# Gated cross- and self-attention block: cross batches and row tiles written out without engine loops, last shift and key copy moved forward

## The reference, cut to what matters

```python
def xattn(q, k, v):                    # q: layernorm(x) (32,100,512); k = v = context (32,722,512)
    qh, kh, vh = heads(q @ wq + bq), heads(k @ wk + bk), heads(v @ wv + bv)
    scores = softmax(einsum('bhqd,bhkd->bhqk', qh, kh), axis=-1)
    return concat(einsum('bhqk,bhkd->bhqd', scores, vh)) @ wo + bo

x = x + tanh(g_xattn[0]) * xattn(layernorm(x), ctx, ctx)
x = x + tanh(g_ffn[0]) * ffn(layernorm(x), g_info, W_qkv, W_proj, b_proj)
# ffn: q, k, v = x @ W_qkv; a cosine of each row's q with a guide row, averaged over heads and
# scaled to 0..1 over all rows, puts the row in one of two classes; attention with two key masks
```

## Time and profile before

| | us |
|---|---|
| median of 3 runs (lowest to highest) | 2854.22 (2852.57 to 2858.64) |
| profiled execution, its time | 2863.41 |
| profiled execution, its span | 2861.5 |
| PE busy in the span | 2642.9 (92%) |
| DVE, ACT, POOL busy | 1829.7, 1336.3, 372.3 |
| granted TensorE clock, mean | 0.961 |

### The profile page before, as it was taken

The page is one execution under the profiler, slowest core; times in us unless marked ns, Lnnn a source line. Parts: engine busy times, 40 slices in busy tenths (PEclk is TensorE's granted clock), DMA queues, the critical chain, the costliest instruction groups (busy, mean ns, idle before and its releaser), DMA issues. The chain is left out here.

```text
span 2861.5 us, 52305 instructions
## 1 busy us (share of the span) xinstructions
PE 2642.9 (92%) x17376; PEld 2361.2 (83%) x17376; DVE 1829.7 (64%) x2869; ACT 1336.3 (47%) x2994; POOL 372.3 (13%) x274
## 2 busy tenths in 40 slices
PE   5799999999999999999999999999949999579999
PEld 5689888988889888888988889888847777478887
DVE  6456676666766666666666766667646677436665
ACT  3235444554445554455544445444433444245654
POOL 0020110000110001110001100011013333100000
PEclk9899999999999999999999999999959999859999
DMA  5545444444544454444554445444339999788982
GB/s 174 176 127 122 120 107 119 118 113 120 119 112 111 120 122 117 105 119 111 121 121 117 119 103 124 119 120 102 92 111 177 187 199 201 152 168 191 194 186 76
DMA packets 367908, 380.02 MB, mean 133 GB/s; under 512 B 127950, under 2 KB 275310, under 8 KB 367726
## 3 DMA queue, kind: packets, MB, share of 16 engines
q1 hardware_dynamic: 317134, 358.18, 53.5%
q10 hardware_dynamic: 50592, 19.06, 3.4%
HBM read 162.57 MB, written 72.57 MB: 82 GB/s over the span
## 5 line engine op out<-in xcount | busy, mean ns | idle before, releaser
L649 DVE TENSOR_TENSOR c_parted<-c_prob,c_parted 128x600 fp32r<-128x600 f32 x512 | 400.9, 783 | 464.0 <-ACT c_prob L590 463.0
L586 ACT ACTIVATE c_parted<-c_pair 128x600 fp32r<-128x600 f32 x512 | 344.4, 673 | 375.5 <-PE c_pair L728 374.6
L635 DVE TENSOR_REDUCE c_peak<-c_pair 100x1 f32<-100x724 f32 x512 | 450.0, 905 | 76.8 <-PE c_pair L710 66.4
L532 POOL TENSOR_TENSOR c_ct_lo<-e_stage,c_ct_hi 128x722 fp32r<-128x722 f32 x128 | 224.7, 1757 | 1766.0 <-ACT c_ct_hi L561 1766.0
L742 PE MATMUL c_mix<-c_parted,c_v 128*66 128x200 f32 (+1 forms) x3072 | 379.0, 260 | 16.5 <-DVE c_q_stack L640 16.4
L728 PE MATMUL c_pair<-c_q_stack,c_k_stack 100*128 100x100 f32 (+1 forms) x3072 | 391.0, 264 | 0.0
L89 PE MATMUL c_work<-c_ct_hi,w_wk_hi 128*128 128x362 f32 (+1 forms) x1024 | 366.0, 357 | 20.1 <-POOL c_ct_lo L532 16.0
L728 PEld LDWEIGHTS c_pair<-c_q_stack,c_k_stack 100*128 100x128 f32 (+1 forms) x3072 | 375.2, 188 | 6.7
L568 ACT ACTIVATE c_v<-c_work 128x512 fp32r<-128x512 f32 x192 | 115.6, 602 | 527.2 <-PE c_work L91 527.2
L742 PEld LDWEIGHTS c_mix<-c_parted,c_v 128*66 128x66 f32 (+1 forms) x3072 | 327.2, 139 | 37.5 <-DVE c_q_stack L640 25.6
L89 PE MATMUL c_work<-w_wv_hi,c_ct_hi 128*128 128x512 f32 (+1 forms) x768 | 317.2, 413 | 34.4 <-issue 28.6
(11 more groups left out here) (162 smaller groups left out, 4155.6 us busy)
## 6 DMA issues: line engine op xcount, KB each, us to landing
c_k_stack<-c_k_hi SPq DMA_DIRECT2D x1024, 90.2 KB, 2.2
e_stage<-in_ctx SPq DMA_DIRECT2D x32, 1444.0 KB, 6.2
c_k_stack<-c_k_lo SPq DMA_DIRECT2D x512, 90.2 KB, 2.2
c_q_stack<-q_parts ACTq DMA_DIRECT2D x186, 100.0 KB, 3.2
mix_parts<-c_mixed SPq DMA_DIRECT2D x64, 200.0 KB, 3.2
r_parts<-mix_parts SPq DMA_DIRECT2D x50, 256.0 KB, 4.2
s_q_stack<-qk_parts SPq DMA_DIRECT2D x16, 800.0 KB
s_k_stack<-qk_parts SPq DMA_DIRECT2D x16, 800.0 KB
```

The costliest lines, as they stand in the source:

```text
L532: pool.tensor_tensor(ct_lo[odd][:, k, :], columns[:, k, :], ct_hi[odd][:, k, :], ALU.subtract).then_inc(ct_lo_done, 1)
L586: act.activation(parted[i % PR][:, :, 0, :].rearrange("p (a t) s -> p a t s", a=2), logits, ACT.Exp).then_inc(exp_hi_done, 1)
L635: dve.tensor_reduce(peak[:, i:i + 1], pair[i % 2][0:S, :, 0:HALF], AX.XY, ALU.max).then_inc(peak_done, 1)
L649: dve.tensor_tensor(p[:, :, 1, :], prob[i % 2][:], p[:, :, 0, :], ALU.subtract).then_inc(p_lo_done, 1)
```

## The change

Four edits. The three engine loops over batches, and those of PE, ACT and DVE over row tiles, become straight code: every batch and tile is written out, with constants where registers were. The fourth shift moves from behind scores 1 to the end of the front part, ahead of the first keys piece. In the row stage ACT's `keys(t)` moves ahead of `split_attn(t + 2)` and `query_root(t)`.

```diff
@@ front_plan
-    return plan + held[:2] + [("scores", 0, 0)] + held[2:]
+    return plan + held[:2] + [("scores", 0, 0)] + held[2:] + [("shift", KT - 1, 0)]
@@ batch_plan
-        if h == 1:
-            plan.append(("shift", KT - 1, 0))
@@ stage_cross, all_batches
-            body(0, 0, True, True)
-            with engine.Fori(0, B // 2 - 1) as u:
-                body(u * 2 + 1, 1, True)
-                body(u * 2 + 2, 0, True)
-            body(B - 1, 1, False)
+            for b in range(B):
+                body(b, b % 2, b < B - 1, b == 0)
@@ stage_rows, scalar, body
                 queries(t, before > 0)
+                keys(t)
                 if more_attn:
                     split_attn(t + 2)
                 query_root(t)
-                keys(t)
                 values(t, before > 0)
@@ stage_rows, scalar
-            with act.Fori(2, TILES - 2) as t:
+            for t in range(2, TILES - 2):
@@ stage_rows, vector
-            with dve.Fori(2, TILES - 2) as t:
+            for t in range(2, TILES - 2):
@@ stage_rows, tensor
-            with pe.Fori(2, TILES - 1) as t:
+            for t in range(2, TILES - 1):
```

## The result

| us | before | after |
|---|---|---|
| median of the runs (lowest to highest) | 2856.43 (2852.57 to 2858.64) | 2789.38 (2779.96 to 2798.39) |
| profiled execution, its span | 2861.5 | 2796.6 |
| mean granted clock in it | 0.961 | 0.965 |
| PE, DVE, ACT busy in it | 2642.9, 1829.7, 1336.3 | 2628.1, 1826.2, 1334.5 |
| first matmul of batch 1 to that of batch 31 | 1812.8 | 1748.8 |

The change is faster: ratio 0.976, 95% interval 0.9734 to 0.9785, 67 us between the medians. One single execution among all the kernels here, 3261.57 us at a granted clock of 0.74 with keys ahead alone, was far slower than every other and is left out of that kernel's numbers. The lower half of the table splits the profiled span by the matmuls that open and close each part; I call the last two the row stage and the self stage throughout, and every experiment is split in the same way.

A forecast was written before the change was run, and what follows sets the result against it. PE, busy 92% of the span, was taken to bound the kernel; 44.3 + 18.6 + 12.3 + 2.6 = 77.8 us gave 2785.6 from 2863.4, and most of the median's 9.2 us offset gave 2779, range 2765 to 2798.

The forecast's parts named there:

- Terms 1 and 2: Cross stage: straight code removes PE's branch stalls and half-clock stretches, 44.3 us; the earlier fourth shift ends mix 0's wait, 18.6.
- The zero for fetching straight code: All engines: fetching new instructions in every batch was costed at nothing, since an engine fetches ahead of its need.
- The fetch rival: Cross stage: DVE or ACT stops once per batch for a fetch, PE behind it; 122 us more, 2901; chance 0.03.
- the moved wait: Cross batches: PE waits as much further on, for DVE's maxima or stacked keys; batch stays 58.95, time 2798; chance 0.05.
- Term 3: Batch 31: mix 0's wait goes and the clock stays full, 2.0 + 9.3 + 1.0 = 12.3 us; bounds 0.9 to 14.
- one of my own signs of a wrong forecast: Profile after: the forecast is wrong if batch 31 is at granted clock 0.50.
- The rival of the slow tail: Batch 31: the clock falls all the same, from PE's small holes behind ACT's exps; 2790; chance 0.13.
- Term 4: Row stage: earlier keys let PE run ahead once until DVE's attention split, 2.6 us gained; bounds -2 to 13.
- The rival that all 13.2 us would go: Row stage: parts land faster once PE's stores leave earlier, so PE's whole wait for copies goes; 2768; chance 0.06.

The follow-up runs named there:

- keys ahead alone: Kernel before with only ACT's key copies moved ahead of its attention split in the row stage: 2858.65 us, ratio 1.0003.
- The batches alone: Kernel before with only the cross stage's batches written out, shift and row stage as before: 2806.33 us, ratio 0.9813.
- the full fill: The change with unread matmuls in batch 31, four ahead of mix 0 and two ahead of each other mix: 2792.61 us.
- TensorE alone: The change with cross batches written out on TensorE only, ACT and DVE given back their loops: 2787.70 us, ratio 0.9748.
- the two fills: The change with four unread matmuls ahead of mix 0 of batch 31, 2786.72 us; with two more ahead of each other mix, 2792.61 us.
- the warming: The change with 50 and 20 unread identity matmuls on TensorE around the self stage's first scores: 2782.67 us, ratio 0.9756.
- the two warmed kernels: Unread self-stage matmuls added to the change, 2782.67 us; and, with four ahead of batch 31's mix 0, to its cross stage with before's row stage, 2782.70 us.
- the cross stage alone: The change with before's row stage, its loops and its order of ACT's copies: 2776.12 us, ratio 0.9737.
- the kernel with less to load: The change, from row tile 4 on loading 8 of 128 partitions of the second set of mixed parts: 2773.69 us, ratio 0.9706.

## Why the prediction was right, and where it was not

The sign, the range (2765 to 2798) and the place of most of the gain were right; the median is 10 us above the forecast. By the steps:

**Terms 1 and 2**, the branches and the shift, 62.3 us between batches 1 and 31 (44.3 and 30 times 0.6): measured 64.0. The pieces bear out both sizes. The batches alone gave 45.3 against 44.3, the half-clock stretches with them, and from there the change took 18.7 more by the shift (1767.5 to 1748.8), 0.62 a batch. The zero for fetching straight code held too: the empty list of waits shows it. (I had called the 158 fetches of the earlier trace rows PE's; that row names a queue and no engine.) By the Trainium skill (Runtime: NRT & Kernel Launch, Instruction fetch mechanics) straight code crosses its blocks mostly unseen, and a taken branch to code outside the blocks at hand waits for its fetch. The trace agrees: no wait of PE in 30 straight batches, and 3.95 us for TensorE's taken branch. The fetch rival (2901) and the moved wait (2798) are out: all batches are at 58.3 to 58.6.

**Term 3**, batch 31, 12.3 us: in the profiled execution of the change 1.2, and there one of my own signs of a wrong forecast stands, batch 31 at 0.50. In the other kernels with the shift ahead it is 13. The step said that with the shift ahead mix 0 would have no gap and no reason would show for the clock to fall. A gap of 0.69 us stays, because I took the order of batch 14 for that of batch 31, where DVE's split of the values stands right before the shift. The effect on the clock is nevertheless as I had it, in most executions: of the ten profiles with the shift ahead nine kept 1.00 through the heads (batch 31 at 44.3 to 44.5 us, 50.6 with the full fill), and the change's own is the one that did not; of the four without it all fell (57.4 to 58.8). That is 13 to 14 us against my 12.3. The rival of the slow tail (2790) describes the one profile that I was shown, not the usual one, and it names another cause: its small holes behind ACT's exps are not there, since the 0.69 us is PE's only idle stretch over 0.15 us in that batch. That the median, 2789.38, is so near its 2790 is then a coincidence, as far as the other profiles tell. The same 0.69 us and the same matmuls gave both outcomes, so neither decides it by itself; what does is not shown, and I take it for chance between executions. The Trainium skill (TensorE: Matmul & The Clock Gate, Part 1) says that with one kernel the point at which the clock rises varies from run to run. The traces go further: with the same code in this stage it fell in one profile, 1.5 us behind the wait, and not in others. That a full-width fill in front of mix 0 makes the full clock certain was not shown: the three profiles with it kept the clock, but six of the seven without it did too.

**Term 4**, the row stage, +2.6: this is the step that failed in every profile with both edits, and by more than that of the change shows (-0.9). "PE gains 2.7 us once" was to come from running ahead of the split. PE's wait for ACT's copies went, the wait for the split took its place, and the tiles stayed near 13.3, all as I wrote. But the split itself comes later. With the two edits together the row stage took 376.3, 383.5, 378.2, 385.6 and 381.1 us (the change, and the kernels on it with TensorE alone, the two fills and the warming; mean 380.9). With before's row stage it took 375.4, 369.4, 372.8, 371.7 and 369.4 (mean 371.7). The two groups don't overlap, if barely (375.4 the longest of the one, 376.3 the shortest of the other), so in the profiles the edits cost some 9 us. The times say so less clearly: without the edits the median is 2776 in place of 2789, but single times overlap, and of the two warmed kernels, run side by side, the one without the edits is no faster (2782.70 and 2782.67). Each edit by itself, on the cross stage of before, costs nothing that can be measured (375.7 and 373.6); neither was tried alone on the new cross stage.

Two parts of the 9 us can be seen. First, from the stage's first join to its fifth it takes 52.1 to 54.4 us where keys go ahead and 49.7 to 51.2 where they don't, some 3 us. I put it down to ACT's key copy, 1 us, which stands in front of the split in the tiles in which everything waits for the first rows. I had named that (down to -2) and set it too low. Secondly, single tiles are late. Waits of the row stage (2090 to 2390 us), first of the kernel with TensorE's batches alone, which has both edits:

```profile
POOL r_attn L936 <- DMA r_parts<-inverses: 184.8, 21, 14.5
...
DVE r_at_lo L1078 <- ACT r_at_hi L978: 78.5, 22, 8.8
...
PE r_mixed L89 <- DVE r_at_lo L1078: 12.2, 6, 5.8
```

and of the cross stage alone, which has neither:

```profile
POOL r_attn L931 <- DMA r_parts<-inverses: 171.3, 21, 9.8
...
DVE r_at_lo L1073 <- ACT r_at_hi L973: 38.1, 21, 3.0
...
PE r_turned_q L1195 <- ACT r_qkv L992: 10.8, 20, 1.7
```

The wait removed, some 11 to 13 us of PE, gave nothing back. What replaced it, the same total in fewer and longer waits (5.8), comes from late joins. The longest of them, in the kernel with both: windows of an ordinary load of parts, of the late one, and of the time until it had landed, then POOL's join and PE.

```profile
2187.50:2193.50 6.00, 5.41 (x24) 4.09 (x23) 5.03 (x11) 1.50 (x3) 0.00 (x0) 1.00 1.11 319
2201.50:2207.50 6.00, 5.40 (x24) 4.09 (x23) 4.83 (x11) 1.72 (x4) 0.00 (x0) 1.00 0.98 290
2207.50:2213.30 5.80, 5.62 (x31) 4.54 (x29) 0.91 (x4) 2.61 (x4) 0.00 (x0) 1.00 1.04 105
```

```profile
2213.37 1.26 POOL L936 TENSOR_TENSOR r_attn<-r_parts 128x512 f32<-128x512 f32 x1 [14.46 <-DMA r_parts<-inverses]
...
2218.91 0.80 PE L89 MATMUL r_mixed<-r_w_hi,r_at_hi 128*128 128x512 f32 x1 [5.79 <-DVE r_at_lo L1078]
```

The DMA engines are as busy as ever (share 1.04) and move a third (105 GB/s): single packets of 512 bytes took up to 3.1 us there, and one of 2048 bytes 4.5, against 0.03 us for the usual one of 512. The join comes 19.6 us behind the last, and PE stands 5.8 us. Joins over 18 us apart beyond the first four occur in three of the five kernels with both edits, and in none of the five with before's row stage. Slow packets are in every kernel's row stage: from 80 us behind its start to 5 us before its end 186 to 232 of them take over 2 us with before's row stage, and 231 to 257 with both edits. Why they are slow, and why there are more with the two edits, I did not find; the kernel with less to load has such tiles too (19.5). The rival that all 13.2 us would go (2768) is out.

**The sum** was 77.8 us; the two profiled spans differ by 64.9. The cross stage gave 1.7 more than its 62.3, batch 31 in that profile gave 11.1 less than its term, and the row stage 3.5 less. So the forecast came near because the errors are small against 62, and not because they cancel. Of the 10 us by which the median lies above 2779, 2 are the kernel before, whose median moved from 2854.22 to 2856.43 with a fourth run. For an execution that keeps its clock in batch 31 the terms would be 64.0 + 13 - 9 = 68, and 67 were measured. I don't know what share of the change's executions keeps the clock, so this is a check of size and no proof.

## What to carry to other kernels

Where TensorE is the full engine, look for waits that the profile puts down to issue behind a loop's branch, and write that engine's loop out. It is the one whose turn costs; the loops of engines with idle time can stay. Before an engine's wait is taken away in a stage, find the loop that sets the stage's pace: if the wait stands beside that loop, the edit may bring nothing, as each of the two did here, or disturb the loop, as both together did in the profiles; so try such edits singly and together. When a change's profile shows a stage at half clock, look at a second profile before calling it the rule.

## What the runs showed of the hardware that I had not expected

- The same code, two outcomes for the clock, in two places of the span. Behind the same wait of 0.69 us in batch 31 the granted clock fell in one profile of seven, at a price of 12 us (56.2 against 44.3). And in the self stage, whose code is the same in all kernels but the two warmed ones, the clock rose 67 to 70 us behind the row stage's last matmul (stage 378 to 380 us) in eight profiles and 86 to 89 us behind it (385 to 389) in four, before and after among them. These two steps, of 12 and of 8 us, are of the size of the spread of single times (2780 to 2798 for the change).
- Filler matmuls brought the clock up while they ran (it was at 1.00 for the 20.5 us shown above), but it fell again in the work behind them, in which TensorE was busy for 12.28 of 17 us.
- The DMA engines' busy share does not tell how much they move: 1.11 at 319 GB/s and 1.04 at 105 GB/s, 20 us apart in one stage.
